# One decoder layer over 16 batches: x1's norm ahead of the last stage's statistics, row scalings later, the next rows' norm on ScalarE

## What is computed

```python
# self-attention: 16 heads of 16, q and k normalised per head, a bias by distance, causal
x = x + attn(layernorm(x))        # inside: rms_norm -> softmax(q k^T + bias) v Wo + x -> rms_norm -> relu(z W1) W2
# cross-attention to ctx: 8 heads of 32, softmax minus sigmoid(lambda) * softmax
x = x + xattn(layernorm(x), ctx)  # inside: layernorm(query + attn) -> relu FFN -> layernorm
# 8 experts; each row takes the one whose centroid is nearest to its normed value
x = x + moe(layernorm(x))         # xn = rms_norm(.) * scale; out = down_e(a * silu(g)) for that expert, plus the normed input
```

## Time and profile before

| | |
|---|---|
| median of 3 runs | 1432.47 us (1429.6 to 1434.39) |
| the profiled execution | 1430.63 us, span of its core 1428.8 us, mean TensorE clock 0.961 |
| TensorE matmul busy | 1275.9 us, 89% |
| VectorE, ScalarE, GpSimd busy | 766.8 (54%), 583.0 (41%), 390.7 us (27%) |
| chain that ended last | TensorE 75%, VectorE 10%, ScalarE 8%, issue 5%, GpSimd 1% |

### The profile page before, as it was taken

How to read it: one execution, slowest core, us unless ns; L and a number is a source line. 1 busy time by engine, 2 the same in 40 slices (tenths; PEclk the granted TensorE clock), 3 DMA queues, 4 the chain that set the end, 5 groups by cost and what they waited for, 6 DMA issues and landing times.

```text
span 1428.8 us, 27261 instructions
## 1 busy us (share of the span) xinstructions
PE 1275.9 (89%) x8838; PEld 929.8 (65%) x8839; DVE 766.8 (54%) x2053; ACT 583.0 (41%) x1253; POOL 390.7 (27%) x680
## 2 busy tenths in 40 slices
PE   6588999999999999999999999999987449999997
PEld 4365776767777776767777777767765325555554
DVE  5645566676766666676666666676643241121111
ACT  3424436363545536363544536363522212222221
POOL 2311121212141221213141221213122124444443
PEclk9598999999999999999999999999999669999999
DMA  8300000000000000000000000000054002112111
GB/s 273 97 8 9 16 1 31 1 29 0 29 29 0 29 0 29 0 29 0 29 29 0 29 0 29 0 29 22 2 192 177 30 22 62 53 56 60 59 55 38
DMA packets 44135, 56.69 MB, mean 40 GB/s; under 512 B 6486, under 2 KB 38016, under 8 KB 44097
## 3 DMA queue, kind: packets, MB, share of 16 engines
q1 hardware_dynamic: 37824, 41.23, 8.8%
q0 software_dynamic: 5616, 14.43, 3.5%
q10 hardware_dynamic: 656, 0.52, 0.1%
HBM read 40.44 MB, written 16.65 MB: 40 GB/s over the span
## 4 chain that ended last, share of the span: by engine, by line
PE 75%; DVE 10%; ACT 8%; issue 5%; POOL 1%; DMA 0%; ACTq 0%; DVEq 0%; SPq 0%; POOLq 0%
PE bank L1337 69%; PE bank L1372 2%; ACT a_p L725 2%; ACT shared L730 2%; PE bank L1519 2%; DVE a_p L1140 2%; DVE shared L1114 1%; PE bank L1664 1%; DVE a_sq L1108 1%; ACT shared L759 1%; ACT b_qh L659 1%; DVE a_split L1084 0%; DVE a_split L1083 0%; DVE shared L1291 0%; DVE a_split L1082 0%
## 5 line engine op out<-in xcount | busy, mean ns | idle before, releaser
L1337 PE MATMUL bank<-shared 128*128 128x256 f32 (+4 forms) x2242 | 447.8, 380 | 44.9 <-ACT shared L670 13.8
L1337 PEld LDWEIGHTS bank<-shared 128*128 128x128 f32 (+2 forms) x2242 | 318.1, 173 | 125.5 <-issue 31.5
L1140 DVE TENSOR_TENSOR a_p<-a_p,eb 128x385 f32<-128x385 f32 x256 | 126.2, 556 | 89.5 <-ACT a_p L725 89.5
L1337 PE MATMUL bank<-up,shared 128*128 x312 | 144.5, 606 | 11.0 <-issue 11.0
L725 ACT ACTIVATE a_p<-bank 128x385 f32<-128x385 f32 x256 | 105.1, 503 | 42.0 <-PE bank L1337 41.9
L869 POOL TENSOR_SCALAR a_rz<-a_ms 128x2 f32<-128x2 f32 x16 | 3.1, 191 | 431.7 <-ACT a_sq L736 431.7
L1337 PE MATMUL bank<-a_xnT,w 128*128 128x256 f32 x512 | 114.7, 382 | 1.4 <-ACT a_xnT L622 1.4
L1337 PE MATMUL bank<-w,a_hT 128*128 128x256 f32 x512 | 113.1, 379 | 0.0
L1314 DVE TENSOR_TENSOR shared<-bank,shared 128x512 f32<-128x512 f32 x39 | 27.0, 692 | 154.4 <-ACT shared L757 84.7
L622 ACT COPY a_xnT<-bank 128x512 f32<-128x512 f32 x32 | 18.8, 587 | 220.2 <-PE bank L1372 220.2
L1337 PEld LDWEIGHTS bank<-a_xnT,w 128*128 128x128 f32 x512 | 96.0, 190 | 18.1 <-issue 3.4
(11 more groups left out here) (206 smaller groups left out, 2037.9 us busy)
## 6 DMA issues: line engine op xcount, KB each, us to landing
up<-in_L_ffn_up_w SPq DMA_DIRECT2D x8, 1024.0 KB, 14.4
x_in<-in_x SPq DMA_DIRECT2D x16, 256.0 KB, 2.7
shared<-in_ctx SPq DMA_DIRECT2D x16, 256.0 KB, 3.0
rows_x<-shared SPq DMA_DIRECT2D x16, 256.0 KB, 2.9
rows_skip<-shared SPq DMA_DIRECT2D x16, 256.0 KB, 3.1
down<-in_L_ffn_down_w SPq DMA_DIRECT2D x8, 512.0 KB, 12.5
toep<-a_hT SPq DMA_DIRECT2D x1, 3072.0 KB, 10.2
eb<-toep SPq DMA_DIRECT2D x4, 512.0 KB, 6.2
```

What stands on the lines that cost most here:

```text
L1140: tt(a_p[:, n_ % NPA], a_p[:, n_ % NPA], eb[:, n_], ALU.mult).then_inc(sig["a_p"], 1)
L1337: return mm(out, lhsT=lhsT, rhs=rhs, start=first, stop=last, **kw)
```

## The change

Six moves, on four engines:

1. ScalarE: `scaled_rows` (line 633) goes from between A's two squares to between hidden(1) and hidden(2).
2. ScalarE: line 652 (residual rows c_x2) goes from the turn's start to after the evacuation of B's maxima, ahead of the copy of x1 (line 710).
3. VectorE: line 1031 goes from the turn's start into `low_q`, ahead of b_ql.
4. The next batch's norm a_xl moves from VectorE (line 994 called at 1176) to ScalarE, after A's last ReLU, as x times rstd plus (-mean times rstd); GpSimd computes that bias in two more steps of a_norms (9 in place of 7).
5. VectorE: x1 and its statistics come before the statistics of c_x2; b_xl stays last.
6. GpSimd: b_norm comes before c_norms.

```diff
--- before.py
+++ after.py
@@ -368,7 +368,7 @@
 
     PER_BATCH = {
 
-        "a_loaded": 16, "a_stats": T, "a_mv": T, "a_norms": 7, "a_xl": T, "a_kept": 1,
+        "a_loaded": 16, "a_stats": T, "a_mv": T, "a_norms": 9, "a_xl": T, "a_kept": 1,
         "a_squares": T, "a_sumsq": T, "a_rn": RN_STEPS, "a_hi": 2 * T, "a_lo_q": T, "a_lo_k": T, "a_p": H0,
         "a_p_used": H0 // GROUP, "a_rec": 3 * C, "a_ms": T, "a_rz": 2, "a_xy": 1,
 
@@ -643,14 +643,6 @@
                 for t in range(T):
                     ps = full(act, it, f"A.qk{t}")
                     nc.scalar.activation(a_sq[:, t], ps[:], ACT.Square).then_inc(sig["a_squares"], 1)
-                    if t == 0 and Cc:
-                        scaled_rows()
-            elif Cc:
-                scaled_rows()
-            if Cc:
-                for t in range(T):
-                    nc.scalar.activation(c_x2[:, t], c_x2[:, t], ACT.Identity, scale=c_sc[:, 7, t:t + 1],
-                                         bias=c_sc[:, 9, t:t + 1]).then_inc(sig["c_rows"], 1)
             if A:
                 if it.first == 1:
                     copy_tops(range(4, 8))
@@ -695,6 +687,9 @@
                     bias_exp()
             if Dd:
                 hidden(1)
+            if Cc:
+                scaled_rows()
+            if Dd:
                 hidden(2)
             for t in range(T):
                 if A:
@@ -704,6 +699,10 @@
                 hidden(3)
             if Bb:
                 evacuate(it, "B.max", b_nmT[:].rearrange("p c s -> p (c s)"))
+            if Cc:
+                for t in range(T):
+                    nc.scalar.activation(c_x2[:, t], c_x2[:, t], ACT.Identity, scale=c_sc[:, 7, t:t + 1],
+                                         bias=c_sc[:, 9, t:t + 1]).then_inc(sig["c_rows"], 1)
             if Bb:
                 if Dd:
                     after(act, "x1_kept2", dd)
@@ -740,6 +739,16 @@
                     nc.scalar.activation(a_hT[:, 2 * n:2 * n + 2].rearrange("p j s -> p (j s)"), ps[:],
                                          ACT.Relu).then_inc(e_sem(f"A.h{n}"), 1)
 
+            if "P" in it.stages:
+                p = it.batch("P")
+                after(act, "a_norms", p)
+                if A:
+                    taken(act, it, "A.z")
+                    after(act, "a_xy", a)
+                for t in range(T):
+                    nc.scalar.activation(a_xl[:, t], x_in[:, t], ACT.Identity, scale=a_sc[:, 1, t:t + 1],
+                                         bias=a_sc[:, 7, t:t + 1]).then_inc(sig["a_xl"], 1)
+
         each(act, turn)
 
 
@@ -825,6 +834,9 @@
             after(pool, name, batch, 6)
             if name == "a_norms":
                 pool.tensor_scalar(sc[:, 6], sc[:, 4], 1e-6, None, ALU.mult).then_inc(sig[name], 1)
+                for t in range(T):
+                    pool.tensor_scalar(sc[:, 7, t:t + 1], mv[:, t, 0:1], sc[:, 1, t:t + 1], -1.0, ALU.mult,
+                                       ALU.mult).then_inc(sig[name], 1)
             else:
                 pool.tensor_tensor(sc[:, 6], sc[:, 5], sc[:, 1], ALU.mult).then_inc(sig[name], 1)
                 pool.tensor_scalar(sc[:, 7], sc[:, 1], 1.0, None, ALU.add).then_inc(sig[name], 1)
@@ -881,11 +893,12 @@
             if Dd:
                 after(pool, "c_mv", dd)
                 layer(c_mv, c_rs, "c_norm", dd, 1e-5)
+            if A:
+                after(pool, "b_mv", a)
+                layer(b_mv, b_rs, "b_norm", a, 1e-5)
+            if Dd:
                 after(pool, "c_mv2", dd)
                 layer_then_rms(c_mv2, c_sc, "c_norms", dd, 1e-5)
-            if A:
-                after(pool, "b_mv", a)
-                layer(b_mv, b_rs, "b_norm", a, 1e-5)
 
         each(pool, turn)
 
@@ -1025,11 +1038,6 @@
         def turn(it):
             A, Bb, Dd, Cc = (st in it.stages for st in "ABDC")
             a, b, dd, c = (it.batch(st) for st in "ABDC")
-            if Cc:
-                after(dve, "c_norms", c)
-                for t in range(T):
-                    dve.scalar_tensor_tensor(c_rows[:, t, 0:D], c_x2[:, t], c_mv2[:, t, 0:1], vecs[:, FSC],
-                                             ALU.subtract, ALU.mult).then_inc(sig["c_xs"], 1)
 
             def nearest():
 
@@ -1094,6 +1102,11 @@
                 low("B.k", 1, b_kl, b_kh)
 
             def low_q():
+                if Cc:
+                    after(dve, "c_norms", c)
+                    for t in range(T):
+                        dve.scalar_tensor_tensor(c_rows[:, t, 0:D], c_x2[:, t], c_mv2[:, t, 0:1], vecs[:, FSC],
+                                                 ALU.subtract, ALU.mult).then_inc(sig["c_xs"], 1)
                 if Bb:
                     low("B.q_", 2, b_ql, b_qh)
 
@@ -1168,12 +1181,6 @@
                 tt(b_f[:], ps[:].rearrange("p (t n) -> p t n", n=D), d_q[:], ALU.add).then_inc(e_sem("D.out"), 1)
                 taken(dve, it, "D.out")
                 stats(b_f, c_st, c_mv, "c_stats", "c_mv", dd)
-            if "P" in it.stages:
-                after(dve, "a_norms", p, 2)
-                if A:
-                    taken(dve, it, "A.z")
-                    after(dve, "a_xy", a)
-                shifted(a_xl, x_in, a_mv, a_sc[:, 1], "a_xl")
             if Dd:
                 after(dve, "c_norm", dd)
                 for t in range(T):
@@ -1185,8 +1192,6 @@
                     after(dve, "c_gain", dd, t + 1)
                     dve.scalar_tensor_tensor(c_x2[:, t], b_f[:, t], c_rs[:, 1, t:t + 1], x1_keep2[:, t], ALU.mult,
                                              ALU.add).then_inc(sig["c_x2"], 1)
-                after(dve, "c_x2", dd)
-                stats(c_x2, c_st, c_mv2, "c_stats2", "c_mv2", dd)
             if A:
                 ps = full(dve, it, "A.out")
                 after(dve, "a_xy", a)
@@ -1199,6 +1204,10 @@
                 ins.then_inc(e_sem("A.out"), 1)
                 taken(dve, it, "A.out")
                 stats(x1, b_st, b_mv, "b_stats", "b_mv", a)
+            if Dd:
+                after(dve, "c_x2", dd)
+                stats(c_x2, c_st, c_mv2, "c_stats2", "c_mv2", dd)
+            if A:
                 after(dve, "b_norm", a)
                 shifted(b_xl, x1, b_mv, b_rs[:, 1], "b_xl")
             if it.first == 1:
```

More of the change, by code:

```diff
@@ L883, in turn @@
                 layer(c_mv, c_rs, "c_norm", dd, 1e-5)
-                after(pool, "c_mv2", dd)
-                layer_then_rms(c_mv2, c_sc, "c_norms", dd, 1e-5)
             if A:
@@ L888, in turn @@
                 layer(b_mv, b_rs, "b_norm", a, 1e-5)
+            if Dd:
+                after(pool, "c_mv2", dd)
+                layer_then_rms(c_mv2, c_sc, "c_norms", dd, 1e-5)
         each(pool, turn)
```

## The result

The changed kernel takes 1436.17 us, the median of 20 runs (1433.62 to 1440.3), beside 1430.34 us for the kernel before in 20 runs on the same chips (1428.13 to 1435.06). The ratio is 1.0041, 95% interval 1.003 to 1.0051: slower by 5.8 us. The profiled execution took 1439.84 us, with a span of 1437.7 us and a mean TensorE clock of 0.961.

The account below looks back on a forecast made before the run. TensorE was taken to bound the kernel, its matmuls busy 89% of the span. Terms 12.7 + 1.8 - 6.4 - 3.5 = +4.6 us on the median 1432.47 gave 1437.1 us, bounds 1434.3 to 1442.8, range 1430 to 1446.

Parts of the forecast that it names:

- likeliest case: Whole kernel: the forecast itself, +4.6 us to 1437.1 us; 72%, of which 40 for slower and 32 for the same.
- start-up: Turn 0: a_xl on ScalarE queues behind copies of bias maxima, first transposes come later; +1.8 us, bounds 1.6 and 2.6.
- turn 17: Drain: b_xl takes 0.74 us, the 3.50 us wait shrinks, the clock stays up; -6.4 us, bounds -7.0 and -3.9.
- the rest: Everything outside the start-up, turns 4 to 16, turn 17 and turn 18 to the distances; predicted 0.
- turn 18: Drain: hidden(0) and hidden(1) go first, the 6.43 us wait disappears; -3.5 us, bounds -5.0 and -2.4.
- full turns: Turns 4 to 16: line 652 uncovered before B's scores costs 0.98 us a turn; +12.7 us, bounds 12.2 and 14.0.
- The three steps costed at nothing: Full turn: line 1031, `scaled_rows` and a_xl fit into idle time in their new places; 0 us.
- That collision: Turn 17: maxima wait for line 1031, which now meets GpSimd's line 858; +0.2 us.
- the estimated 1.5 us for a slower clock behind that wait: Turn 18: TensorE idles 2.7 us, then runs at a slower clock; 1.5 us set against the -5.0.
- the relief reaches the maxima: Rival, full turns: VectorE's chain from b_ql runs 0.96 us earlier, the maxima wait goes; -7.9 us, 1424.6; 12%.
- The late c_norms: Rival, full turns: c_norms or line 1031 late, b_ql slips by up to 0.88 us; +11.4 more, 1448.5; 8%.
- The clock in the full turns: Rival: the clock falls in every full turn after the longer wait before B's scores; +32.5 us, about 1470; 5%.

## Why the prediction came out as it did

The direction and the likeliest case held: 1437.1 us were predicted and 1436.17 measured, +5.8 us against +4.6. Luck has a part in it. The two times lie so close because the kernel before came out at 1430.34 us and not at 1432.47. And the prediction's errors offset each other: 2.0 us too little for the start-up, 0.5 each in turn 17 and in the rest, against 1.6 too much in turn 18 and 0.3 in the full turns.

*The full turn.* Right in place, mechanism and size: 12.7 us predicted, 12.4 measured, 0.96 us a turn against 0.98. The wait stands where it was said to, 1.20 us for the exponentials. The step alone gives 1.20 as well, and taken to a covered place it gives the 64.12 us turn back. The three steps costed at nothing (line 1031, `scaled_rows`, a_xl on ScalarE) are at nothing in that turn. a_xl runs from 540.17 to 541.26 at the end of turn 8, and the next copy of ScalarE comes at 546.15, 4.9 us later, where five were forecast.

*The start-up.* Mis-sized: +1.8 us predicted with a bound of 2.6, +3.8 measured. The end of the step was placed well: transposes at 19.4 were forecast, and the five profiles with turn 0's a_xl on ScalarE show 18.80 to 19.32. The base was off. 17.64 was itself a late execution; the four other kernels with turn 0's a_xl on VectorE have 16.56 to 16.80. And what ScalarE waits for is in two of the five profiles GpSimd's longer chain (by 0.63 us in the first, 0.30 in another), not its own queue of copies. In the five profiles of each kind the first transposes start on average at 18.96 and 16.86, 2.1 us apart. By the reckoning from the medians turn 4 starts at 214.6 to 216.4 in the five of the one kind and at 212.1 to 214.1 in those of the other: means 215.6 and 212.9, 2.7 apart, and 3.8 apart for the two kernels compared here. So 2 us of it are the late transposes. What makes up the other 0.6 to 1.7 us stays open. The profiles give no sign that a later start brings the lower clock: from the first transposes to turn 4 the five with ScalarE's a_xl take 197.0 us on average and the other five 197.2, and the last part of turn 1 takes more than 21 us in one of the former and in three of the latter.

*Turn 17.* -6.4 predicted, -5.9 measured, but the title "where the reordering pays" was wrong. Each part is there in the trace: b_xl 0.74, the 3.50 us wait down to 0.68, the clock up. Undoing the reordering costs only 0.9 us of the 5.9, and doing the moves without it gives 5.0. In the prediction's own terms: the 1.6 us of b_xl is real but not a net gain, since GpSimd's long step only meets another VectorE pair instead (old line 1031, 2.53 us; it takes 1.10 where the order is put back), and TensorE then waits 1.22 us for b_ql. That collision was seen and costed at +0.2 us; it is the term that was mis-sized. And the wait of 1.77 us was not enough to bring the clock down: with it in place and 0.67 behind it the 16 matmuls took 3.73 us, at full speed; with 2.53 behind it, in the experiment that moves line 652 alone, they took 5.22. (The Trainium skill, GPSIMD Engine Reference, Specifications, says that GpSimd's SBUF interfaces are shared with VectorE for two-port modes and for two SBUF inputs. The traces agree in that the scalar_tensor_tensor pair, which reads two tiles, takes 2.53 us beside GpSimd steps of 1.09 us. The tensor_scalar pair takes 2.34; in which mode it runs, no row shows.)

*Turn 18.* The order of events was right, and the wait of 2.7 us is there with 2.82. -3.5 was predicted, -5.05 measured: the estimated 1.5 us for a slower clock behind that wait didn't come, and the bound of -5.0 was the value. That is a matter of the execution. Seven profiles have this order of work of ScalarE and TensorE up to the wait. In six, this one among them, the slower clock falls on the 32 matmuls ahead of the wait (8.79 to 10.03 us), the wait takes up the loss, and the turn lasts 16.2 us. In the seventh, line 652 behind the exponentials, it falls on the 8 behind the wait, and the turn lasts 17.69: there the estimated 1.5 us came. What decides between the two, no run here shows.

*The rivals.* That the relief reaches the maxima falls with the wait of 0.95 us, which didn't change. The late c_norms falls with 2 us to spare. The clock in the full turns stayed at 1.00 although TensorE waits 1.20 us in each, right behind transposes. (The Trainium skill, TensorE: Matmul & The Clock Gate, What's actually happening, ties the slower clock to idleness that lasts; at 1.00 throughout, the wait and the transposes did not bring it about here.)

## What to carry to other kernels

In an in-order queue a step's price is that of its slot: the same 0.99 us pair cost nothing behind hidden(1), 0.35 us a turn behind the exponentials and 0.96 us a turn ahead of them. Before moving a step, look for the idle time of its engine that another engine ends, and put the step there; a slot that is free in the steady turns may cost in the drain (here 1.0 us, ahead of hidden(2)), so the two can be chosen apart. And where one profile gives the base of a small term, look at that base in a second execution of the same code first.

## What the hardware showed that was not expected

The start-up of the same code varied by more than this change is worth. Five profiles with turn 0's norm on VectorE start turn 4 at 210.91 to 217.05 us, the five with it on ScalarE at 213.99 to 220.03, and the two ends of each range come from kernels that are the same up to turn 4. Between two executions of the changed kernel 3.9 of 5.3 us lay in one stretch of turn 1, at a granted clock of 0.79 in one (0.50 in its first 5 us) and 1.00 in the other.

A VectorE pair on SBUF that begins 0.07 us after a 1.09 us tensor_tensor of GpSimd takes 1.6 us longer (0.74 to 2.34, and 0.88 to 2.53), more than the whole length of GpSimd's step. In turn 17 GpSimd has three such steps in a row, and each instruction of the pair lasts until 0.15 to 0.3 us behind the end of one of them: 1051.18 and 1052.36 beside GpSimd's 1051.03 and 1052.20 in the kernel before, 1074.60 and 1075.83 beside 1074.32 and 1075.55 in the changed one. The pair pays for two steps.
